# The FFN of both batches in one set of operations on four token tiles, behind the second residual

## The reference, cut to what matters

```
t = t + attn(ln(t))          # 8 heads of 16, softmax with a recency bias, projection by w_out
t = t + ffn(ln(t))
x = from_tokens(t)           # back to channels x tokens

def ffn(x):                  # x: (2, 256, 128), all integer work on each token by itself
    hot = x > 0.5
    lo, hi, sa = first hot index in channels 16..31, 20..35, 24..39   (0 if none)
    val = lo + 16 * hi
    res = clip((val << sa) & 255 if mark and SHL else val >> sa if mark and SHR else 0, 0, 255)
    out = x;  out[32 + (res & 15)] += 2 * active;  out[36 + (res >> 4)] += 2 * active
```

## Time and profile before

| what | value |
|---|---|
| median of 3 runs | 58.28 us (58.28, 57.55, 58.33) |
| the profiled execution | 57.51 us, its span 55.6 us |
| VectorE busy | 42.4 us (76%), 143 instructions |
| TensorE busy | 41.6 us (75%), 314 matmuls |
| ScalarE busy | 29.0 us (52%) |
| GpSimd busy | 17.0 us (31%) |
| mean granted TensorE clock | 0.968 |
| chain that ended last | VectorE 41%, TensorE 35%, ScalarE 12%, waiting for nothing visible 7% |
| output transfers | 2 of 128 KB, 1.7 us from issue to landing |

### The profile page before, as it was taken

How to read it: one execution, slowest core, us unless ns; L and a number is a source line. 1 busy time by engine, 2 the same in 40 slices (tenths; PEclk the granted TensorE clock), 3 DMA queues, 4 the chain that set the end, 5 groups by cost and what they waited for, 6 DMA issues and landing times.

```text
span 55.6 us, 1008 instructions
## 1 busy us (share of the span) xinstructions
PE 41.6 (75%) x314; PEld 26.6 (48%) x314; DVE 42.4 (76%) x143; ACT 29.0 (52%) x64; POOL 17.0 (31%) x46
## 2 busy tenths in 40 slices
PE   0997999994590769716994997899597897994420
PEld 0334889570340655313881593499282445741310
DVE  1798864399959449999979999989848998559720
ACT  4403463963376497616999339429679060066010
POOL 4788250699998920000000004040000620013000
PEclk9999975599999999999999999999999999999999
DMA  0482400000000000000000000000000000002002
GB/s 0 129 248 33 21 1 0 0 0 0 0 6 0 0 0 0 12 0 0 0 0 0 0 0 0 0 0 0 0 18 0 0 0 0 0 0 94 0 0 94
DMA packets 1564, 0.91 MB, mean 16 GB/s; under 512 B 404, under 2 KB 1560, under 8 KB 1560
## 3 DMA queue, kind: packets, MB, share of 16 engines
q1 hardware_dynamic: 1104, 0.79, 4.6%
q10 hardware_dynamic: 456, 0.08, 2.0%
HBM read 0.60 MB, written 0.26 MB: 16 GB/s over the span
## 4 chain that ended last, share of the span: by engine, by line
DVE 41%; PE 35%; ACT 12%; issue 7%; DVEq 0%; ACTq 0%
PE ps L899 6%; PE ps L918 6%; DVE negmax L674 5%; PE ps L901 4%; ACT probs L437 4%; DVE stacks L487 3%; PE ps L868 3%; PE ps L934 3%; DVE q_parts L582 3%; DVE stacks L590 3%; DVE k_parts L584 2%; DVE hs L545 2%; PE ps L780 2%; PE ps L773 2%; ACT stacks L415 2%
## 5 line engine op out<-in xcount | busy, mean ns | idle before, releaser
L674 DVE TENSOR_REDUCE negmax<-ps 128x2 f32<-128x512 f32 x16 | 10.7, 674 | 1.2 <-PE ps L868 1.1
L747 PE MATMUL ps<-warm 128*128 128x512 bf16 x32 | 9.6, 442 | 1.3 <-DVE warm L484 1.3
L437 ACT ACTIVATE probs<-ps 128x1024 f32<-128x1024 f32 x8 | 8.0, 1022 | 3.6 <-PE ps L901 3.5
L310 POOL TENSOR_TENSOR on<-pvq,rsum 128x256 f32<-128x256 f32 x3 | 1.9, 623 | 22.6 <-DVE rsum L605 22.6
L899 PE MATMUL ps<-stacks 128*128 128x256 f16 x32 | 7.0, 273 | 1.0 <-ACT stacks L415 1.0
L868 PE MATMUL ps<-stacks 128*128 128x256 f16 x32 | 6.0, 273 | 1.0 <-ACT stacks L411 0.7
L901 PE MATMUL ps<-qmk,ident 128*128 128x256 f16 (+1 forms) x32 | 6.6, 246 | 0.0
L747 PEld LDWEIGHTS ps<-warm 128*128 128x128 bf16 x32 | 3.3, 111 | 5.4 <-issue 2.3
L918 PE MATMUL ps<-probs,v_aug 128*32 128x256 f32 x64 | 4.3, 384 | 1.0 <-ACT probs L437 0.8
L411 ACT COPY stacks<-ps 64x1024 f16<-64x1024 f16 x4 | 3.9, 1005 | 1.4 <-PE ps L844 1.3
L899 PEld LDWEIGHTS ps<-stacks 128*128 128x128 f16 x32 | 3.1, 98 | 1.6 <-ACT stacks L415 1.3
(11 more groups left out here) (142 smaller groups left out, 90.3 us busy)
## 6 DMA issues: line engine op xcount, KB each, us to landing
x_sb<-in_x_dram SPq DMA_DIRECT2D x1, 256.0 KB, 2.8
out_dram<-y_sb SPq DMA_DIRECT2D x2, 128.0 KB, 1.7
wqkv_sb<-in_L_attn_w_qkv_dram SPq DMA_DIRECT2D x1, 192.0 KB, 2.9
wout_sb<-in_L_attn_w_out_dram SPq DMA_DIRECT2D x1, 64.0 KB, 3.0
bout_bc<-in_L_attn_b_out_dram ACTq DMA_DIRECT2D x1, 64.0 KB, 4.2
params<-in_L_conv_ln_w_dram ACTq DMA_DIRECT2D x1, 1.0 KB
params<-in_L_conv_ln_b_dram ACTq DMA_DIRECT2D x1, 1.0 KB
params<-in_L_conv_dt_w_dram ACTq DMA_DIRECT2D x1, 0.5 KB
```

The source lines that it names most:

```text
L437: act.activation(probs[:, 2 * c:2 * c + 2, :, :].rearrange("p h k q -> p (h k q)"), s2_ps[c % 2].rearrange("p a n -> p (a n)"), ACT.Exp, s ...
L674: dve.tensor_reduce(negmax[:, g, :, quadrant], s1_ps[h % 2].rearrange("p (q k) -> p q k", q=HALVES), AX_X, ALU.max, negate=True).then_inc( ...
L747: pe.matmul(ps[:, bank, :], warm[:, 0:P], warm[:], start=True, stop=True)
```

## The change

`find_channels(b)` is split: `test_channels(b)` compares the two tiles of a batch with their thresholds, and one `find_channels()` does the rest for four tiles. `look_up()` and `one_hots()` also run once, on four tiles. On VectorE `test_channels(0)` stands behind `by_dim(3)`, `test_channels(1)` behind `token_stats(1)`, and then the three common functions. The output of each tile has a PSUM bank of its own (banks 2 to 5, 128 columns each). On TensorE `plain(0)` and `plain(1)` stand between the first warm-up matmuls and `project(1)`, the seven warm-up matmuls behind `project(1)` write bank 6, then `plain(2)`, `plain(3)`, and `marked` for the four tiles. ScalarE copies tiles 0 and 2, VectorE tiles 1 and 3, each at the very end; each batch's transfer waits for both copies.

```diff
--- before.py
+++ after.py
@@ -168,7 +168,7 @@
         mT_ps = ps[:, 7, 0:HW // 2].bitcast(F16)
         pv_ps = [ps[:, bank, 0:HW] for bank in (6, 6, 6, 7)]
         proj_ps = [ps[:, 0, 0:HW].rearrange("p (t c) -> p t c", c=C), ps[:, 0:2, HW:HW + C]]
-        y_ps = [ps[:, 4, 0:HW].rearrange("p (t c) -> p t c", c=C), ps[:, 4:6, HW:HW + C]]
+        y_ps = ps[:, 2:6, 0:P]
 
         s_x = sem("x_in")
         s_wqkv, s_wout, s_params, s_bc, s_bout = sem("wqkv_in"), sem("wout_in"), sem("params_in"), sem("bc_in"), sem("bout_in")
@@ -200,6 +200,7 @@
         s_proj, s_t2 = sem("proj_done"), sem("t2_ready")
         s_nfm, s_thr, s_eqz = sem("t3_coefs"), sem("threshold_ready"), sem("one_hots_zeroed")
         s_t1b, s_fmv, s_frs = sem("t1b_ready"), sem("fvar_ready"), sem("frs_ready")
+        s_above = sem("channels_tested")
         s_t3, s_eq2 = sem("t3_ready"), sem("one_hots_ready")
         s_yT, s_y, s_out = sem("yT_done"), [sem(f"out{b}_ready") for b in range(B)], sem("out_done")
 
@@ -225,7 +226,7 @@
             sp.dma_start(wout_sb[:], w_out).then_inc(s_wout, 16)
             yv = out.rearrange("b c h w -> c b (h w)")
             for b in range(B):
-                sp.wait_ge(s_y[b], (1, HALVES)[b])
+                sp.wait_ge(s_y[b], HALVES)
                 sp.dma_start(yv[:, b, :], y_sb[:, b, :]).then_inc(s_out, 16)
             sp.wait_ge(s_out, 16 * B)
 
@@ -465,11 +466,10 @@
             plus_normalised(0)
             token_scale(1)
 
-            act.wait_ge(s_yT, HALVES)
-            act.copy(y_sb[:, 0, :].rearrange("p (t c) -> p t c", c=P), y_ps[0]).then_inc(s_y[0], 1)
             plus_normalised(1)
-            act.wait_ge(s_yT, HALVES + 1)
-            act.copy(y_sb[:, 1, 0:P], y_ps[1][:, 0, :]).then_inc(s_y[1], 1)
+            for b in range(B):
+                act.wait_ge(s_yT, 2 * b + 1)
+                act.copy(y_sb[:, b, 0:P], y_ps[:, 2 * b, :]).then_inc(s_y[b], 1)
 
         @block.vector
         def _(dve):
@@ -627,43 +627,44 @@
                 for t in tiles(b):
                     dve.bn_aggr(fmv[:, t, :], fst[:, t, :]).then_inc(s_fmv, 1)
 
-            def find_channels(b):
-
-                ts = slice(HALVES * b, HALVES * (b + 1))
+            def test_channels(b):
+
                 dve.wait_ge(s_thr, b + 1)
                 dve.wait_ge(s_fmv, 2 * b + 2)
-                link(*[dve.tensor_scalar(above[:, t, :], t2[:, t, 0:SHR + 1], fmv[:, t, 0:1], thr[:, t:t + 1],
-                                         ALU.subtract, ALU.is_gt) for t in tiles(b)])
-                one = above[:, ts, LO:LO + D]
-                windows = bass.AP(one.tensor, one.offset, [one.ap[0], one.ap[1], [WIN, 3], [1, D]])
-                link(dve.tensor_tensor(cand[:, ts, :, :], windows,
-                                       index_less_16[:].unsqueeze(1).unsqueeze(1).broadcast_to([P, HALVES, 3, D]),
+                for t in tiles(b):
+                    dve.tensor_scalar(above[:, t, :], t2[:, t, 0:SHR + 1], fmv[:, t, 0:1], thr[:, t:t + 1],
+                                      ALU.subtract, ALU.is_gt).then_inc(s_above, 1)
+
+            def find_channels():
+
+                dve.wait_ge(s_above, NT)
+                one = above[:, :, LO:LO + D]
+                spans = bass.AP(one.tensor, one.offset, [one.ap[0], one.ap[1], [WIN, 3], [1, D]])
+                link(dve.tensor_tensor(cand[:], spans,
+                                       index_less_16[:].unsqueeze(1).unsqueeze(1).broadcast_to([P, NT, 3, D]),
                                        ALU.mult),
-                     dve.tensor_tensor(either[:, ts], above[:, ts, SHR], above[:, ts, SHL], ALU.max),
-                     dve.tensor_scalar(sgn[:, ts], above[:, ts, SHL], 2.0, -1.0, ALU.mult, ALU.add))
-                link(dve.tensor_reduce(first[:, ts, :], cand[:, ts, :, :], AX_X, ALU.min))
-
-                link(dve.tensor_scalar(idx[:, ts, :], first[:, ts, :].bitcast(U32), 15, None, ALU.bitwise_and),
-                     dve.scalar_tensor_tensor(twos[:, ts], either[:, ts], 2.0, above[:, ts, 0], ALU.mult, ALU.mult))
-
-            def look_up(b):
-                ts = slice(HALVES * b, HALVES * (b + 1))
+                     dve.tensor_tensor(either[:], above[:, :, SHR], above[:, :, SHL], ALU.max),
+                     dve.tensor_scalar(sgn[:], above[:, :, SHL], 2.0, -1.0, ALU.mult, ALU.add))
+                link(dve.tensor_reduce(first[:], cand[:], AX_X, ALU.min))
+
+                link(dve.tensor_scalar(idx[:], first[:].bitcast(U32), 15, None, ALU.bitwise_and),
+                     dve.scalar_tensor_tensor(twos[:], either[:], 2.0, above[:, :, 0], ALU.mult, ALU.mult))
+
+            def look_up():
 
                 link(*[dve.tensor_scalar(amt[:, t:t + 1], idx[:, t, 2:3], sgn[:, t:t + 1], 16.0, ALU.mult, ALU.add)
-                       for t in tiles(b)],
-                     dve.scalar_tensor_tensor(val[:, ts], idx[:, ts, 1], 16.0, idx[:, ts, 0], ALU.mult, ALU.add))
-                link(dve.tensor_tensor(shifted[:, ts], val[:, ts], amt[:, ts], ALU.logical_shift_left))
-                link(*[dve.tensor_scalar(nib[:, ts, k], shifted[:, ts], 16 + 4 * k, 15, ALU.logical_shift_right,
+                       for t in range(NT)],
+                     dve.scalar_tensor_tensor(val[:], idx[:, :, 1], 16.0, idx[:, :, 0], ALU.mult, ALU.add))
+                link(dve.tensor_tensor(shifted[:], val[:], amt[:], ALU.logical_shift_left))
+                link(*[dve.tensor_scalar(nib[:, :, k], shifted[:], 16 + 4 * k, 15, ALU.logical_shift_right,
                                          ALU.bitwise_and) for k in range(2)])
-                link(dve.tensor_tensor(eq[:, ts, :, :],
-                                       iota_i[:].unsqueeze(1).unsqueeze(1).broadcast_to([P, HALVES, 2, D]),
-                                       nib[:, ts, :].unsqueeze(3).broadcast_to([P, HALVES, 2, D]), ALU.is_equal))
-
-            def one_hots(b):
-                ts = slice(HALVES * b, HALVES * (b + 1))
+                link(dve.tensor_tensor(eq[:], iota_i[:].unsqueeze(1).unsqueeze(1).broadcast_to([P, NT, 2, D]),
+                                       nib[:].unsqueeze(3).broadcast_to([P, NT, 2, D]), ALU.is_equal))
+
+            def one_hots():
                 dve.wait_ge(s_eqz, 1)
-                dve.tensor_tensor(eq2[:, ts, :, 0:D], eq[:, ts, :, :],
-                                  twos[:, ts].unsqueeze(2).unsqueeze(3).broadcast_to([P, HALVES, 2, D]), ALU.mult)\
+                dve.tensor_tensor(eq2[:, :, :, 0:D], eq[:],
+                                  twos[:].unsqueeze(2).unsqueeze(3).broadcast_to([P, NT, 2, D]), ALU.mult)\
                    .then_inc(s_eq2, 1)
 
             def largest(h):
@@ -719,24 +720,24 @@
             odd_shifts(3)
             token_stats(0)
             dve.wait_ge(s_consts, 4)
-            find_channels(0)
             by_query(2)
             invert(2)
-            look_up(0)
             by_dim(2)
             by_query(3)
             invert(3)
             normalise(3)
             by_dim(3)
-            one_hots(0)
+            test_channels(0)
             residual(1)
             token_stats(1)
-            find_channels(1)
-            look_up(1)
-            one_hots(1)
-
-            dve.wait_ge(s_yT, NT)
-            dve.tensor_copy(y_sb[:, 1, P:HW], y_ps[1][:, 1, :]).then_inc(s_y[1], 1)
+            test_channels(1)
+            find_channels()
+            look_up()
+            one_hots()
+
+            for b in range(B):
+                dve.wait_ge(s_yT, 2 * b + 2)
+                dve.tensor_copy(y_sb[:, b, P:HW], y_ps[:, 2 * b + 1, :]).then_inc(s_y[b], 1)
 
         @block.tensor
         def _(pe):
@@ -935,35 +936,19 @@
                                      start=(g == 0), stop=(g == 1))
                 last.then_inc(s_proj, 1)
 
-            def output(b):
-                if b == 0:
-                    pe.wait_ge(s_exp, B * HEADS // 2)
-                else:
-                    pe.wait_ge(s_y[0], 1)
-
-                def plain(t):
-                    pe.wait_ge(s_t3, 2 * b + t + 1)
-                    pe.matmul(y_ps[b][:, t, :], t3[:, 2 * b + t, :], ident[:], start=True, stop=False,
-                              skip_group_check=True)
-
-                def marked(t):
-                    pe.wait_ge(s_consts, 1)
-                    pe.wait_ge(s_eq2, b + 1)
-                    flat = eq2[:, 2 * b + t, :, :].rearrange("p k w -> p (k w)")
-                    for k in range(2):
-                        last = pe.matmul(y_ps[b][OUT_LO:OUT_LO + VW, t, :], flat[:, VW * k:VW * (k + 1)], ident16[:],
-                                         start=False, stop=(k == 1), skip_group_check=True)
-                    last.then_inc(s_yT, 1)
-
-                if b == 0:
-                    for t in range(HALVES):
-                        plain(t)
-                        marked(t)
-                else:
-                    for t in range(HALVES):
-                        plain(t)
```

(25 more changed lines are left out.)

## The result

The changed kernel took 59.81 us (median of 4; 59.70 to 61.43), the kernel before 58.30 (57.55 to 58.50): a ratio of 1.030 with a 95% interval of 1.017 to 1.043, and 1.51 us between the medians. I had said 59.1 us and 58.2 to 59.8. It is slower, and by 0.7 us more than forecast; whether by more than 2% the interval leaves open.

The account below looks back on a forecast made before the run. The prediction took one slackless thread over the last 8.5 us as the bound. Terms -0.18 (ahead of the second residual), +0.60 (ladder) and +0.40 (tail and issue) gave +0.82, hence a median of 59.1 us, range 58.2 to 59.8.

Parts of the forecast that it names:

- What bounds it: Last 8.5 us of the chain: one thread without slack, so each step lengthened behind the second residual is paid in full.
- Ahead of the residual: Before the second residual: VectorE gains 0.72 us without look_up(0), but TensorE's queue leaves only -0.18.
- The ladder: VectorE's short steps before the one-hot matmuls, widened to four tiles: more elements and two more amt instructions, +0.60 us.
- The tail: One-hot matmuls, copies and both transfer issues at the end: +0.40 us, low end +0.24.
- The clock: Rival, chance 0.28: granted clock falls before the one-hots, 0.4 us later, total +1.22, 59.5 us.
- the high end: At the output transfers: +0.8 us if the second also queues behind the first one's data.
- The sum: Whole kernel: -0.18 + 0.60 + 0.40 = +0.82 us.
- From the profile to the median: Whole kernel: profiled execution 57.51 + 0.82 = 58.33 us; it stood 0.77 below the median, so 59.1 predicted.
- VectorE's gain arrives: Rival, chance 0.07: projection ends near 47.1, -0.7 us ahead of the second residual, sum -0.2, 58.1 us.
- steps doubled: Rival, chance 0.10: short VectorE steps double in duration, 1.3 us instead of 0.6, sum +1.5, 59.8 us.
- the tail is absorbed: Rival, chance 0.11: one-hots and issue cost no more than 0.24 us, some amt overlap, sum +0.5, 58.8 us.

Follow-up runs that it names:

- half_ladder: Changed kernel with find_channels, look_up and one_hots on batch 1's two tiles alone, batch 0's search left out; median 59.10 us, ratio to the kernel before 1.020.
- plain_behind: Changed kernel with plain(0) and plain(1) behind project(1) instead of ahead of it; median 59.26 us, ratio to the kernel before 1.015.
- steady: Kernel before with fifteen more warm-up matmuls in TensorE's idle stretches between 13 and 25 us; median 57.62 us, ratio 0.990.
- tail_only: Kernel before with SyncE waiting for both batches' outputs before issuing the first transfer; median 58.92 us, ratio 1.009.
- steady_b: Second run of steady, the kernel before with fifteen more warm-up matmuls; median 57.46 us, ratio 0.999.
- wide_warm: Changed kernel with six more warm-up matmuls ahead of plain(2) and three behind plain(3); median 59.40 us, ratio to the kernel before 1.023.
- again: Changed kernel, unedited, timed again; median 59.60 us, ratio to the kernel before 1.019.
- again2: Changed kernel, unedited, timed once more as reference; median 59.79 us, ratio to the kernel before 1.007.
- two_queues: Changed kernel with batch 1's output transfer issued on ScalarE's queue instead of SyncE's; median 59.65 us (kernel before 58.38).
- one_transfer: Changed kernel with one 256 KB output transfer behind all four copies instead of two of 128 KB; median 60.15 us, ratio to the kernel before 1.021.
- wide_steady: Changed kernel with the fifteen warm-up matmuls of steady between 13 and 25 us; median 59.72 us (kernel before 58.38).
- wide_steady_b: Second run of wide_steady, the changed kernel with fifteen more warm-up matmuls; median 59.39 us, ratio to the kernel before 1.015.
- wide_steady_warm: Changed kernel with the fifteen warm-up matmuls plus wide_warm's six and three around plain(2) and plain(3); median 58.67 us, ratio to the kernel before 1.016.

## Why the prediction was wrong, step by step

**What bounds it.** Right: the thread behind the residual passed every term on to the end in full (half_ladder 0.58 to 0.57, plain_behind 0.44 to 0.45).

**Ahead of the residual.** -0.18 predicted, -0.17 measured, and for the reason given: TensorE's order. plain_behind gave the four records back. That it fits to 0.01 is in part luck of the profile before: the old residual stands at +4.44 in before and steady, but at +4.28 in tail_only and +4.27 in steady_b, whose code is the same up to there. Against those two the change gains nothing ahead of the residual, and costs 1.31 from V to the end (13.41 against 12.10 in steady_b).

**The ladder.** +0.60 predicted, 5.57 - 4.97 = 0.60 measured. `cand` took 0.36 and four `amt` 0.58, as forecast.

**The tail.** +0.40 predicted; with the clock at 1.0 wide_warm gives 3.37 - 2.85 = +0.52. The second issue came 1.16 behind the one-hots' start, inside the 1.14 to 1.22. What was missing is that the span then ends 2.2 us after that issue in place of 2.09, with the first transfer just ahead of it; I had put that in the high end alone. This term was mis-sized by 0.12.

**The clock.** This step of the sum failed: I put the fallen clock at nothing, as a rival with 0.28, and based the time on the full one. The granted clock was 0.50 at the one-hots, and their eight records took 1.01 us, in after, again, again2, plain_behind, half_ladder, two_queues, one_transfer and wide_steady. One profile with the same order of warm-ups kept it, wide_steady_b, where the eight took 0.79 with one gap among them:

```profile
54.18:54.98 0.80, 0.79 (x8) 0.48 (x8) 0.22 (x1) 0.36 (x2) 0.00 (x0) 1.00 0.00 0
```

As evidence against the fall I had the 5 us at 13.20 to 18.20 that kept 1.00, but these held 2.34 us of matmul time, while the change leaves TensorE only four records of `plain`, 0.84 us, in the 4.1 us ahead of the one-hots. The Trainium skill warns (TensorE: Matmul & The Clock Gate, "Why this matters for your kernels") that a gap without matmuls between bursts brings the lower clock back, and eight of these nine profiles agree in the outcome. The fall at 7.73, which I took to agree, does not speak for it: it came behind 18 matmuls that were busy 2.50 of 2.87 us. The price was overrated, 0.19 measured and 0.4 predicted: the records took 1.01 us and not 1.24, so that the last copy is only 0.2 late against the issue step.

**The sum.** -0.17 + 0.60 + 0.52 + 0.19 = 1.14 of the 1.15 measured; predicted were 0.82, and 1.22 in the clock's rival. On the median before that is 59.45.

**From the profile to the median.** The other 0.36 us, the largest part of the 0.69 by which the forecast was off, lie here. The prediction added its sum to the median as if both kernels' executions spread alike, and gave no reason. Seven of 22 executions of the changed kernel fell in the latest of its three groups, 8 of 74 before; with the shares of before, the differences by group give 1.2 us. What puts V late arises ahead of V, in code that both kernels share. Up to 0.16 may come of the shorter last stretch that steady_b shows, if unprofiled executions of the kernel before have it too. Whether the change shifts the shares, or 22 executions fell so by chance, stays open; no edit of this study aimed at it.

Of the other rivals, "VectorE's gain arrives" (-0.7 ahead of the residual), "steps doubled" (+1.3 on the ladder) and "the tail is absorbed" (+0.24) are refuted by the stages: -0.17, +0.60, +0.52.

## What to carry to other kernels

Fewer and wider operations save nothing where the second set was hidden in a wait: moving hidden work behind the last dependency puts its elements on the path, and here 11 VectorE instructions fewer came with 1.15 us more. Cost a step that is freed on one engine against the next engine's queue: 0.72 us of VectorE time became 0.17 because of four records on TensorE, and 0.60 with these behind the projection (plain_behind, +3.84 against +4.44). Compare two profiles from a mark behind which only the change differs; ahead of it profiles differed here by 1.0 to 2.9 us for other reasons.

## What the runs showed of the hardware

- Where the granted clock falls matters more than that it falls: with one fall of 3.4 us at 7.7 us V is 43.4, with one at 19.5 us it is 44.4. Fifteen matmuls of 0.21 us in idle time took 0.8 to 0.95 us off the median of the kernel before, and little off that of the changed one (59.72 and 59.39 against 59.60 to 59.81).
- A granted clock of 1.00 is no proof of full pace: in again, again2 and wide_steady_warm eight f32 records of 128 columns took 2.05 us at 1.00 where they took 1.16 in after. The step from record to record tells the pace.
- A VectorE step of two elements beside GpSimd's multiply ran until the multiply ended: `val` took 0.61 us before (0.15 in the second batch), and in tail_only it slipped past and `shifted` took the wait, 0.46 in place of 0.16. That moved the residual by 0.16 us, with no edit to that stage; the one kernel of steady and steady_b shows both, +4.44 and +4.27. The rows are tail_only's:

```profile
43.62 0.15 DVE L655 SCALAR_TENSOR_TENSOR val<-idx 128x2 uint32<-128x2 uint32 x1
43.80 0.46 DVE L656 TENSOR_TENSOR shifted<-val,amt 128x2 uint32<-128x2 uint32 x1
```

- The last DMA issue of SyncE took 1.54 and 1.75 us in place of 0.34 to 0.43 in two profiles, each with an instruction transfer in that stretch.
